# First attention of a two-layer kernel: two value products placed one block later on TensorE, and one zeroing of the K tile placed later on VectorE

## The reference, cut to what matters

```python
def _L0_xattn_ref(query, key_value, Wq, bq, Wk, bk, Wv, bv, Wo, bo):
    q = (query @ Wq + bq).reshape(B, Nq, H, D).transpose(0, 2, 1, 3)      # H = 16 heads, D = 16
    k = (key_value @ Wk + bk).reshape(B, Nkv, H, D).transpose(0, 2, 1, 3)
    v = (key_value @ Wv + bv).reshape(B, Nkv, H, D).transpose(0, 2, 1, 3)
    attn = jnp.einsum('bhqd,bhkd->bhqk', q, k) * scale
    attn = jnp.clip(attn, -CLAMP, CLAMP)
    attn = jax.nn.softmax(attn, axis=-1)
    ...
    x = jnp.einsum('bhqk,bhkd->bqhd', attn, v).reshape(B, Nq, Cq)
    return x @ Wo + bo
...
x = x + _L0_xattn_ref(_layernorm(x, axis=-1), ctx_768, ...)
x = x + _L0_ffn_ref(_layernorm(x, axis=-1), ...)
...
```

## Time and profile before

| what | value |
|---|---|
| runs of the kernel before | 918.64, 918.67, 931.78; median 918.67 |
| the profiled execution, device time | 917.04 |
| its span, first to last instruction | 915.1 |
| outside of the span | 1.94 |
| TensorE, VectorE, ScalarE, GpSimd busy | 85%, 77%, 61%, 32% of the span |
| mean granted TensorE clock | 0.927 of full speed |
| attention blocks, first scores of block 0 to last value product | 47.87 to 318.3 |

### The profile page before, as it was taken

The page is one execution under the profiler, slowest core; times in us unless marked ns, Lnnn a source line. Parts: engine busy times, 40 slices in busy tenths (PEclk is TensorE's granted clock), DMA queues, the critical chain, the costliest instruction groups (busy, mean ns, idle before and its releaser), DMA issues.

```text
span 915.1 us, 21761 instructions
## 1 busy us (share of the span) xinstructions
PE 775.8 (85%) x8198; PEld 584.1 (64%) x8198; DVE 702.4 (77%) x1455; ACT 557.9 (61%) x1156; POOL 291.6 (32%) x256
## 2 busy tenths in 40 slices
PE   3788999999998677899899999996647998869995
PEld 1456666666665464778477777783224886459994
DVE  7767888888888897876667776647886987767766
ACT  6657767677674346543655556646977775763542
POOL 6244544535442524050522220005721221532400
PEclk9789999999999778999999999999558999789997
DMA  6434444445543356242477766532210000200002
GB/s 174 109 75 101 118 100 108 108 107 125 140 106 90 94 189 227 90 128 58 125 200 192 197 194 175 151 89 60 74 37 1 1 1 10 85 0 3 3 1 72
DMA packets 75661, 89.60 MB, mean 98 GB/s; under 512 B 22069, under 2 KB 62276, under 8 KB 75584
## 3 DMA queue, kind: packets, MB, share of 16 engines
q1 hardware_dynamic: 68752, 80.50, 31.9%
q0 software_dynamic: 6144, 7.42, 3.3%
q10 hardware_dynamic: 688, 0.66, 0.3%
HBM read 72.87 MB, written 15.43 MB: 97 GB/s over the span
## 4 chain that ended last, share of the span: by engine, by line
PE 50%; DVE 20%; ACT 9%; issue 8%; POOL 6%; DMA 5%; SPq 1%; DVEq 0%; ACTq 0%; POOLq 0%
PE ps L1213 11%; PE ps L1200 9%; PE ps L575 4%; PE ps L547 3%; PE ps L475 3%; PE ps L528 3%; ACT area L1738 2%; PE ps L377 2%; PE ps L619 2%; PE ps L2298 2%; DVE p L563 2%; PE ps L2309 2%; PE ps L1814 2%; ACT area L1705 1%; DVE m L533 1%
## 5 line engine op out<-in xcount | busy, mean ns | idle before, releaser
L533 DVE TENSOR_REDUCE m<-ps 100x2 f32<-100x722 f32 x128 | 114.9, 899 | 48.1 <-PE ps L528 46.8
L554 ACT ACTIVATE p<-ps 128x800 f32<-128x800 f32 x128 | 106.6, 833 | 47.6 <-PE ps L547 45.7
L1262 ACT ACTIVATE hT<-ps,cols 128x500 f32<-128x500 f32 (+1 forms) x96 | 62.5, 651 | 96.6 <-PE ps L1200 85.8
L563 DVE SCALAR_TENSOR_TENSOR p<-p 128x600 f32<-128x600 f32 x128 | 106.1, 829 | 1.0 <-ACT p L554 1.0
L1213 PE MATMUL ps<-w_h,hT_h 128*125 128x256 f16 (+1 forms) x384 | 104.7, 273 | 1.8 <-DVE x L1309 1.2
L1213 PE MATMUL ps<-w_h,hT_l 128*125 128x256 f16 (+1 forms) x384 | 104.7, 273 | 0.0
L1213 PE MATMUL ps<-w_l,hT_h 128*125 128x256 f16 (+1 forms) x384 | 104.7, 273 | 0.0
L1269 DVE TENSOR_TENSOR hT_l<-hT,hT_h 128x500 f16<-128x500 f32 (+1 forms) x96 | 62.4, 652 | 54.6 <-ACT hT_h L1263 54.3
L1105 POOL DMA_INDIRECT xe<-tokens,slot_of x32 | 44.4, 1387 | 146.3 <-PE ps L1223 99.0
L1200 PE MATMUL ps<-xe_h,w_h 128*128 128x500 f16 (+1 forms) x192 | 71.4, 372 | 16.0 <-ACT hT_h L1263 6.2
L1200 PE MATMUL ps<-xe_l,w_h 128*128 128x500 f16 (+1 forms) x192 | 71.1, 370 | 0.0
(11 more groups left out here) (356 smaller groups left out, 2099.7 us busy)
## 6 DMA issues: line engine op xcount, KB each, us to landing
stage<-in_ctxT_dram SPq DMA_DIRECT2D x16, 541.5 KB, 6.2
sw<-in_L_ffn_w_dram SPq DMA_DIRECT2D x16, 512.0 KB
sw<-in_L_ffn_w_dram SPq DMA_DIRECT2D x8, 1024.0 KB, 5.9
k_parts<-kp SPq DMA_DIRECT2D x32, 192.0 KB, 3.9
ks<-k_parts SPq DMA_DIRECT2D x32, 192.0 KB
stage<-in_L_xattn_W_f_dram SPq DMA_DIRECT2D x6, 1024.0 KB, 7.7
ctx_f<-in_ctxT_dram SPq DMA_DIRECT2D x16, 270.8 KB, 3.1
ks<-k_parts SPq DMA_DIRECT2D x32, 96.0 KB
```

The source lines that it names most:

```text
L533: v.tensor_reduce(m32[p][:, 2 * i:2 * i + 2], ps[0:T, at:at + 2, 0:KV], AX.X, ALU.max).then_inc(m_max, 1)
L554: s.activation(p32[:, i % HALF, :, :, :].rearrange("p j n t -> p n j t"), ps[:, t_bank(i):t_bank(i) + 2, 0:(KJ + 1) * T].rearrange("p n (j ...
L563: v.scalar_tensor_tensor(probs, probs, 1.0, low, ALU.min, ALU.max).then_inc(a_cv, 1)
L1262: s.activation(hT[:, f % 3, 0:m], bank[2 + f % 2][:, 0:m], ACT.Silu, bias=bias, scale=1.0 / WS)
```

## The change

It moves whole calls and leaves every instruction's work as it is.
- In `a_tensor`, step 1: the first V product of batch b + 1 (`v_tensor`, 12 matmuls) goes ahead of the wait for `m_l` and of the last value product of block b - 1.
- In `a_tensor`: the wait for `m_l` of the next batch's first half and the value product of group 1 go from step 5 to step 6, behind that step's `t_tensor` and `s_tensor`.
- On VectorE: the zeroing of rows 64 to 128 of the first K tile goes from ahead of the split of Wk to behind the first `open_norm`.
- On SyncE: the two stores of K of batch 0 go ahead of the wait for `k_pad` 3 and the load of `floor_k`.

```diff
@@ a_tensor
+                if i == 1 and has(b, 2):
+                    v_tensor(pe, b + 1, q, 0, (k_32, 2 * b + 5))
                 if i == 1:
                     pe.wait_ge(m_l, 2 * b + 2)
                 if i == 1 and from_(b, 1):
                     pv_tensor(pe, b - 1, q, NQ - 1)
-                if i == 1 and has(b, 2):
-                    v_tensor(pe, b + 1, q, 0, (k_32, 2 * b + 5))
...
-                if i == 5 and has(b, 1):
+                if i == 6 and has(b, 1):
                     pe.wait_ge(m_l, 2 * b + 3)
-                if i == 5:
+                if i == 6:
                     pv_tensor(pe, b, p, 1)
@@ block.vector
             v.memset(ks_flat[0][32:64, :].bitcast(F32), MINUS_ONES).then_inc(k_pad, 1)
-            v.memset(ks_flat[0][64:128, :].bitcast(F32), 0.0).then_inc(k_pad, 1)
             v.memset(floor_k[:, :].bitcast(F32), 0.0).then_inc(k_pad, 1)
             split_weight(v, "Wk")
             open_stats(v, 0)
             open_norm(v, 0)
+            v.memset(ks_flat[0][64:128, :].bitcast(F32), 0.0).then_inc(k_pad, 1)
             split_weight(v, "Wq")
@@ block.sync
+            for c in range(CC):
+                k_store(sp, 0, 0, 0, c)
             sp.wait_ge(k_pad, 3)
             sp.dma_start(floor_k[ROW_M:128, :], a["pick_h"][:, H * AP:]).then_inc(floor_in, 16)
-            for c in range(CC):
-                k_store(sp, 0, 0, 0, c)
             k_load(sp, 0, 0, 0)
```

## The result

| | median, us | runs | profiled execution | its span | granted clock |
|---|---|---|---|---|---|
| before | 920.08 | 4 | 917.04 | 915.1 | 0.927 |
| after | 936.58 (934.97 to 942.05) | 4 | 934.97 | 932.0 | 0.918 |

The medians differ by 16.5 us, where 3.1 were forecast. The ratio is 1.020, with a 95% interval of 1.0168 to 1.0231; it is taken from the faster executions alone, so it isn't that of the two medians (1.018). The kernel is slower, and the interval has both sides of 2% in it. The profiled executions are compared span against span (+16.9).

The account below looks back on a forecast made before the run. TensorE, with two short stalls a block, was taken to pace the attention; in the opening it waits for VectorE. Opening -0.4, step 1 +0.57, step 6 +1.95 and last block +1.0 gave +3.1: 921.8 us, range 916.5 to 926.5.

Parts of the forecast that it names:

- Step 5 to 6, the formula: Attention blocks: step 7 starts at exponential 5's start + 3.27 (scores to value product 0.31); +1.95 us over eleven blocks.
- Blocks 0, 1 and 12 I cost at nothing: Step 6 move there: shift covered by TensorE's wait for GpSimd's context part at the next K product; 0 us.
- Rival 3: Held exponential delays ScalarE's context conversion, GpSimd's split and the next block's K product; 4 us more, 926; chance 0.15.
- rival 4: Opening: VectorE's split of Wk blocks GpSimd's context subtraction by a shared port; opening +0.4, total 922.6; chance 0.05.
- Last block, +1.0: Block without maxima: the moved value product no longer fills exponential 5's time and delays the projection's end; +1.0 us.
- Step 1, +0.57: V product in front waits for ScalarE's accumulator read instead; -0.11 or +0.02 to +0.09 a block, +0.57 us in all.
- Opening, -0.4: Wk's split and K products start 2 us earlier, Q follows 0.3 to 0.4 earlier; -0.4 us, ends -1.5 and +0.3.
- It ends near 14.8: Opening: VectorE's normalisation, waiting for ScalarE until 12.9, ends near 14.8 instead of 15.9.
- The 0.70 gap: Opening: idle time ahead of VectorE's zeroing; its return at the new place was the upper end, +0.3 us.
- my 20.1 for the low part of x: Opening: VectorE starts the low part of x at 20.1 instead of 20.43, after zeroing and Wq's split.

Follow-up runs that it names:

- only_step6: Kernel before with only the move of group 1's value product and its wait from step 5 to step 6; 932.82 us, ratio 1.0142.
- before_again: Kernel before run once more, with no edit, for a second profile; 928.02 us, one run.
- step6_value_first: Kernel before with group 1's value product and its wait moved to step 6, between t_tensor and s_tensor; 923.99 us, ratio 1.0019.
- only_step1: Kernel before with only the V product put ahead of the value product in step 1; 922.83 us, ratio 1.0032.
- opening_zero_on_gpsimd: Kernel before with the zeroing of rows 64 to 127 of K's tile given to GpSimd instead of VectorE; 920.79 us, ratio 1.0009.
- opening_only: Kernel before with only the opening's changes: zeroing behind the normalisation, K stores ahead of the wait; 924.73 us, ratio 1.0041.
- step6_fifth_slot: Kernel before with the step 6 move and a fifth p32 slot, so step 6's exponential isn't held by the value product; 932.4 us, ratio 1.0124.

## Why the prediction was wrong

The mechanism of the moved wait was right, the direction too; the size was off by a factor of more than five, and the time lies outside of the range, because the cover that I took for free grew. By its steps:

**Step 5 to 6, the formula: right.** Every link came out within 0.01, but for the 0.31 to the value product, which is 0.40. The term was +1.95 for eleven blocks, of which blocks 3 to 10 make 1.93; only_step6 took 2.6 more there than the first profile of before and 1.9 more than the second. Against the first, block by block, the forecast is off by 0.01 in block 5, 0.04 to 0.08 too low in six, which is the step of 0.40, and 0.26 too low in block 3, whose K product waited 0.38: blocks 6, 4 and 10, to which I had given the least, cost the least (0.05, 0.21 and 0.21).

**"Blocks 0, 1 and 12 I cost at nothing": this is the step that failed.** I took TensorE's wait for GpSimd's context part as a cover, with a chain that "starts before step 5" and so stays as it is. It starts before, but it ends when VectorE lets it, and the order of TensorE's step 6 sets VectorE's gaps. The cover was itself the bound: the split grew by 1.5 us in blocks 0 and 1, the wait for it from 1.14 and 1.28 to 2.45 and 2.50, and TensorE's lower clock behind the longer of them took 1.40 more, which I had at nothing. Together with what the moves cost in each block it is +4.7 in blocks 1 and 2 (block 2 I had counted among the eleven, at -0.22). Rival 3 had the place (the K product waiting for GpSimd's split) and priced 4 us for it, but by the wrong link, a late exponential; there the delay was 0.40 in block 8, where I had said 0.35. Of rival 4's rule I had the row (1.48 beside Wq's low part) and asked only what it does where the change adds a new pair of neighbours on purpose, in the opening. (There GpSimd's subtraction did take 2.46 instead of 1.70 beside the split of Wk, but its K parts came earlier, not later.) The change alters which instructions of VectorE and GpSimd meet in every block.

The Trainium skill (SBUF — State Buffer, "Who interferes with whom") says that a VectorE instruction with two inputs in SBUF and a GpSimd instruction that reads SBUF exclude each other, that the loser blocks fully, and that the order of issue decides. The runs agree that it is a full block and that the order decides, in both directions. They don't agree that it lasts for one instruction: in block 1 the split should have got in behind the first clip, at 78.83, and ended near 79.7; it stayed out over two more clips and the reductions between them, whose inputs are in PSUM, until VectorE paused. In block 8 the split did get in behind the first clip, as that section has it.

**Last block, +1.0.** From exponential 5 to x's first addition it took 6.04 instead of 5.41, +0.63; but before_again took 7.53, with TensorE at a lower granted clock (0.65 from 300 to 320 us, 0.74 in the first profile, 0.81 after), so the profiles neither show this term nor rule it out. What was missed is guard_z, +3.1 on VectorE, of which the block gives 0.8 back ahead of step 5. It hangs on where GpSimd's additions lie when VectorE gets there (2.33 to 3.32 in the five profiles with the move as it was made, 0.18 in the nine others). One of these nine is step6_value_first, which in block 15 has the same order as only_step6, since there are no scores for maxima: so it is the timing that the move brings, and not the order in that block.

**Step 1, +0.57.** Measured in only_step1 +0.10 to +0.19 a block instead of 0.02 to 0.09, so 1.2 to 2.3 over twelve blocks: mis-sized, in part by the two releases above (1.41 for 1.32, 0.85 for 0.79). As a time of the whole kernel it isn't clear of the noise (ratio 0.9996 to 1.0067). The wait I named did take the old one's place.

**Opening, -0.4.** Measured +1.4 to +2.8. Two steps failed. "It ends near 14.8": it ended at 16.25, since the normalisation met GpSimd's work, which before was over when it began (14.54 against 14.60). The 0.70 gap, which I kept as the upper end, came back. With both, my 20.1 for the low part of x becomes 22.3, and 22.06 was measured. A third would have failed next: K's earlier store held ScalarE's cast for 2.36, ahead of Q's input. In the changed kernel VectorE was later still, so it cost nothing there; in opening_zero_on_gpsimd, with the zeroing gone from VectorE, it gave away what was gained.

**The sum.** Opening +1.6, blocks 1 and 2 +4.7, loop +5.4 for both moves (of which the two profiles of before differ by 1.0), last block +3.0, block 0 to be left out. The +3.8 behind the attention stays open: in the same kernel this stretch took 601.59 and 610.78, with a granted clock of 0.93 and 0.88 from 320 to 500 us. It took 601.1 to 610.8 in the eight profiles without the move and 604.5 to 607.8 in the six with it, so none tells what of it is due to the change.

**What the runs say of the spread.** The kernel before gave 912.84 to 931.78 in all its runs but one, which took 1031.59 at a granted clock of 0.739. opening_only shows one source: its blocks 11 to 13 took 7.7 us more than in before, and GpSimd's L611 took 3.42, 3.46 and 3.42 there instead of 1.03. The same lock-out falls on blocks or spares them, apparently by when GpSimd is released there; that I didn't test.

## What to carry to other kernels

Where two engines can shut each other out, a third engine's order matters: before you take a wait away from TensorE, look which gaps of VectorE it made, and what GpSimd did in them. In this kernel the same GpSimd operation took 1.3 or 4.6 beside the same VectorE instructions, so look at it block by block. An idle stretch that you want to use as cover has to be followed to what ends it; if that is a GpSimd operation that takes three times its shortest duration, it is no cover but the next bound. And an idle stretch of TensorE may be paid twice, as its clock can fall behind it. A wait placed where the busy engine would otherwise run through can be worth more than it costs.

## What was not expected of the hardware

- A GpSimd operation of 0.86 us took up to 6.21 (step6_fifth_slot), beside VectorE instructions of 0.76 and 0.9 each. In block 1 of the kernel before it came through at a gap of 0.08 us behind a clip (79.21 to 79.29); in block 8 it came through with no gap.
- A wait of 2.50 us was followed by 3.4 us of TensorE at its lower clock, at a cost of 1.40.
- The reverse: a VectorE operation on 64 elements a partition (0.18) took 3.31 behind three GpSimd instructions in a row; and the normalisation of four times 256 elements 3.12 instead of 1.38.
- In TensorE's order the value product of step 6 starts 0.40 behind the scores, where the projection takes 0.31 behind the same scores.
- The zeroing of 64 x 3072 took 2.62 on VectorE with an idle time of 0.70 ahead of it at either place, and about the same on GpSimd in the opening (2.66).
